# Heads stage without its loop over tiles, and two loads of FP4 codes issued by ScalarE

## The reference, cut to what matters

```python
x = x + cross_attention(layernorm(x), ctx, ctx)        # 512 wide, 256 context rows per sequence
x = x + self_attention(layernorm(x))                   # 16 heads of 128, rotary, causal, 64 tokens per sequence
x = x + ffn(layernorm(x))                              # FP4 weights, 1408 hidden, silu gate, RMS norm of the output
```

## Time and profile before

| what | value |
|---|---|
| median of 3 runs | 1446.46 us (1444.58 to 1448.53) |
| profiled execution | 1445.04 us |
| its span, first to last instruction | 1443.2 us |
| TensorE busy | 1360.7 us (94%), 8964 matmuls |
| VectorE busy | 980.1 us (68%) |
| ScalarE busy | 508.1 us (35%) |
| GpSimd busy | 425.7 us (29%) |
| DMA | 122.53 MB, mean 85 GB/s |
| mean granted TensorE clock | 0.980 of full speed |

### The profile page before, as it was taken

The page is one execution under the profiler, slowest core; times in us unless marked ns, Lnnn a source line. Parts: engine busy times, 40 slices in busy tenths (PEclk is TensorE's granted clock), DMA queues, the critical chain, the costliest instruction groups (busy, mean ns, idle before and its releaser), DMA issues. The chain is left out here.

```text
span 1443.2 us, 24076 instructions
## 1 busy us (share of the span) xinstructions
PE 1360.7 (94%) x8964; PEld 795.3 (55%) x8964; DVE 980.1 (68%) x2176; ACT 508.1 (35%) x1249; POOL 425.7 (29%) x302
## 2 busy tenths in 40 slices
PE   8999999968999899998999999999998499999997
PEld 6666666435666566665667666654443234343433
DVE  6443443447887688776877777738829796969693
ACT  3222222322333333332343333320001483838281
POOL 0000000003333133331333333320302391929292
PEclk9999999989999999999999999999999699999999
DMA  8555555331001100101010000268550000000000
GB/s 323 218 212 211 212 196 193 118 126 54 31 28 47 61 30 31 59 16 60 31 59 30 18 28 31 89 199 244 166 157 1 0 2 29 0 29 0 29 1 30
DMA packets 59459, 122.53 MB, mean 85 GB/s; under 512 B 4312, under 2 KB 37720, under 8 KB 52696
## 3 DMA queue, kind: packets, MB, share of 16 engines
q1 hardware_dynamic: 59352, 121.07, 24.5%
HBM read 95.89 MB, written 25.17 MB: 84 GB/s over the span
## 5 line engine op out<-in xcount | busy, mean ns | idle before, releaser
L931 POOL TENSOR_TENSOR hd_rotated<-hd_products 64x512 f32<-64x512 f32 x64 | 109.3, 1708 | 725.1 <-DVE hd_products L1116 725.1
L184 PE MATMUL psum<-hd_xt_hi,hqk_hi 128*128 128x512 f16 x512 | 195.8, 382 | 1.7 <-DVE hd_xt_lo L1090 1.7
L185 PE MATMUL psum<-hd_xt_lo,hqk_hi 128*128 128x512 f16 x512 | 195.6, 382 | 0.0
L186 PE MATMUL psum<-hd_xt_hi,hqk_lo 128*128 128x512 f16 x512 | 195.2, 381 | 0.0
L1442 POOL TENSOR_TENSOR ff_part<-ff_part 128x512 f32<-128x512 f32 x88 | 127.7, 1465 | 98.0 <-DVE ff_part L1569 97.6
L184 PE MATMUL psum<-hd_wv_hi,hd_xt_hi 128*128 128x256 f16 x512 | 140.3, 274 | 4.6 <-DVE hd_wv_lo L1095 4.6
L1471 PE MATMUL psum<-ff_xt_hi,gu 128*128 128x512 f16 x352 | 133.9, 380 | 8.2 <-DVE w_rows L1607 3.3
L185 PE MATMUL psum<-hd_wv_lo,hd_xt_hi 128*128 128x256 f16 x512 | 140.3, 274 | 0.0
L186 PE MATMUL psum<-hd_wv_hi,hd_xt_lo 128*128 128x256 f16 x512 | 140.2, 274 | 0.0
L1472 PE MATMUL psum<-ff_xt_lo,gu 128*128 128x512 f16 x352 | 133.4, 379 | 0.0
L1569 DVE SCALAR_TENSOR_TENSOR ff_part<-psum,gu_scale,ff_part 128x512 f32<-128x512 f32 x176 | 119.8, 738 | 6.2 <-ACT ff_part L1519 3.6
(11 more groups left out here) (170 smaller groups left out, 2795.0 us busy)
## 6 DMA issues: line engine op xcount, KB each, us to landing
xa_kv_t<-in_ctx_t_dram SPq DMA_DIRECT2D x16, 1024.0 KB, 5.3
xa_kv<-in_ctx_dram SPq DMA_DIRECT2D x16, 1024.0 KB, 4.8
w_rows<-in_head_weights_dram SPq DMA_DIRECT2D x12, 1024.0 KB, 7.5
z_scratch<-hd_z_hi SPq DMA_DIRECT2D x32, 256.0 KB, 2.2
z_scratch<-hd_z_lo SPq DMA_DIRECT2D x32, 256.0 KB, 2.5
w_rows<-z_scratch SPq DMA_DIRECT2D x8, 1024.0 KB, 8.0
hqk_lo<-z_scratch SPq DMA_DIRECT2D x8, 1024.0 KB, 7.7
xn<-in_x_dram SPq DMA_DIRECT2D x8, 512.0 KB, 3.8
```

The costliest lines, as they stand in the source:

```text
L184: pe.matmul(out, lh, rh, start=(first and i == 0), stop=False)
L185: pe.matmul(out, lh, rl, start=False, stop=False)
L186: last = pe.matmul(out, ll, rh, start=False, stop=(final and i == k - 1))
L931: pool.tensor_tensor(rotated[0:HALF, w, 0, :], products[0:HALF, w, 0, :], products[0:HALF, w, 2, :], ALU.subtract)
```

## The change

The heads stage is written out for all four tiles: `for_each_step` no longer takes an engine and has no `Fori`, addresses and counts become constants, and the `nop`s that followed register waits go. In the merge stage the loads of codes 2 and 3 leave SyncE's list and stand at the head of ScalarE's, each behind its wait on `gu_decoded`; SyncE keeps codes 1 and all of z. No arithmetic changes.

```diff
@@ heads_phase
-        def for_each_step(eng, step):
+        def for_each_step(step):
...
-            with eng.Fori(0, NT - 1) as t:
-                tile(t, False)
-            tile(NT - 1, True)
+            for t in range(NT):
+                tile(t, t == NT - 1)
...
-                    sp.nop(nofuse=True)
-                    sp.dma_start(xn[:, :, :], rows_of(s.t * TILE + TILE)).then_inc(x_loaded, 16)
+                    sp.dma_start(xn[:, :, :], rows_of(s.t * TILE + TILE)).then_inc(x_loaded, 16)
                 for h in range(2):
                     banks.wait_moved(sp, s.runs_z, (s.z, h))
-                    sp.nop(nofuse=True)
...
                     banks.wait_moved(pool, s.runs_proj, ("qk"[w], 1))
-                    if not isinstance(s.t, int):
-                        pool.nop(nofuse=True)
...
                     banks.wait_filled(dve, s.runs_scores, s.scores)
-                    dve.nop(nofuse=True)
...
-            for_each_step(nc.tensor, step)
+            for_each_step(step)
@@ merge_phase, sync
-            def load_codes(g):
-                sp.dma_start(codes[g % 2], codes_of(gu_codes, g)).then_inc(gu_loaded[g % 2], 16)
...
             load_z(1, 0)
-            load_codes(1)
+            sp.dma_start(codes[1], codes_of(gu_codes, 1)).then_inc(gu_loaded[1], 16)
...
                 for half in range(2):
                     sp.wait_ge(z_used[half], t - 1 + half)
                     load_z(t, half)
-                    if half == 0:
-                        sp.wait_ge(gu_decoded, t - 1)
-                        load_codes(t)
@@ merge_phase, scalar
+            for g in range(2, KD):
+                act.wait_ge(gu_decoded, g - 1)
+                act.dma_start(codes[g % 2], codes_of(gu_codes, g)).then_inc(gu_loaded[g % 2], 16)
             for n, (_, _, _, hi, _) in enumerate(jobs):
```

More of the change, by code:

```diff
@@ L825, in rows_of @@
         def rows_of(first):
-            return x1_rows[bass.ds(first, TILE), :].rearrange("(b p) d -> p b d", p=P)
+            return x1_rows[first:first + TILE, :].rearrange("(b p) d -> p b d", p=P)
         class Step:
@@ L894, in load_wo @@
                 sp.wait_ge(w_lo_done, t + KD)
-                sp.nop(nofuse=True)
-                sp.dma_start(w_rows[:, 0, :], w_o[:, bass.ds(t * (4 * D), 4 * D)]).then_inc(loaded[0], 16)
+                sp.dma_start(w_rows[:, 0, :], w_o[:, t * (4 * D):(t + 1) * (4 * D)]).then_inc(loaded[0], 16)
             def step(s):
@@ L909, in step @@
                     banks.wait_moved(sp, s.runs_z, (s.z, h))
-                    sp.nop(nofuse=True)
                 for half, z in enumerate((z_hi, z_lo)):
-                    sp.dma_start(z_scratch[half, s.pair * 2:s.pair * 2 + 2, :, bass.ds(s.first_token, TILE)].rearrange("h d t -> d h t"),
+                    sp.dma_start(z_scratch[half, s.pair * 2:s.pair * 2 + 2, :, s.first_token:s.first_token + TILE].rearrange("h d t -> d h t"),
                                  z[:, :, :]).then_inc(small_loaded_z_stored, 16)
@@ L918, in step @@
                         load_wo(s.t + 1)
-            for_each_step(nc.sync, step)
+            for_each_step(step)
         @block.gpsimd
@@ L933, in step @@
                                        ALU.add).then_inc(pool_rotated, 1)
-            for_each_step(nc.gpsimd, step)
+            for_each_step(step)
         @block.tensor
@@ L1065, in step @@
                             act.wait_ge(small_loaded_z_stored, s.a * 32 + 16 * HEADS_SMALL)
-                            act.nop(nofuse=True)
                         act.activation(z_hi[:, h, :], psum_of((s.z, h)), ACT.Identity,
@@ L1076, in step @@
                     act.wait_ge(loaded[0], s.t * 16 + 32)
-                    act.activation(wo_hi[:, bass.ds(s.t * 4, 4), :].rearrange("p n m -> p (n m)"), w_rows[:, 0, :], ACT.Copy,
+                    act.activation(wo_hi[:, s.t * 4:s.t * 4 + 4, :].rearrange("p n m -> p (n m)"), w_rows[:, 0, :], ACT.Copy,
                                    scale=WS).then_inc(wo_hi_done, 1)
@@ L1081, in _ @@
             act.wait_ge(zeros_set, 1)
-            for_each_step(nc.scalar, step)
+            for_each_step(step)
         @block.vector
@@ L1132, in while_exponentials_run @@
                     dve.wait_ge(wo_hi_done, s.t + 1)
-                    if not isinstance(s.t, int):
-                        dve.nop(nofuse=True)
-                    dve.scalar_tensor_tensor(wo_lo[:, bass.ds(s.t * 4, 4), :].rearrange("p n m -> p (n m)"), w_rows[:, 0, :], WS,
-                                             wo_hi[:, bass.ds(s.t * 4, 4), :].rearrange("p n m -> p (n m)"),
+                    dve.scalar_tensor_tensor(wo_lo[:, s.t * 4:s.t * 4 + 4, :].rearrange("p n m -> p (n m)"), w_rows[:, 0, :], WS,
+                                             wo_hi[:, s.t * 4:s.t * 4 + 4, :].rearrange("p n m -> p (n m)"),
                                              ALU.mult, ALU.subtract).then_inc(w_lo_done, 1)
@@ L1164, in step @@
                                                              z_hi[:, h, :], ALU.add, ALU.subtract), (s.z, h))
-            for_each_step(nc.vector, step)
+            for_each_step(step)
 ZW_UNSCALE = 1.0 / (AS * WS)
```

## The result

| kernel | median, us | runs | span of the profiled execution |
|---|---|---|---|
| before | 1445.83 | 1444.58 to 1448.53 (4) | 1443.2 |
| changed | 1428.67 | 1427.44 to 1429.69 (4) | 1425.6 |

The ratio is 0.9878 with a 95% interval of 0.9864 to 0.9892: 17.2 us faster, where 24.8 us were forecast. The time lies 0.3 us inside the upper end of the whole range (1406 to 1429), and outside the forecast's own range (1416 to 1427).

What follows compares the result with a forecast made beforehand. TensorE, busy 94% of the span, bounds the kernel, idling at loop jumps and before the last stage. Gains of 11.8 (loop), 11.9 (23.9 less 12 collision) and 1.1 sum to 24.8 us: 1421 us, range 1406 to 1429.

Steps and rivals of the forecast that it cites:

- the forecast's own range: Whole kernel: 1416 to 1427 us, for z stalls of 6 to 17 us in the merge stage; chance 0.52.
- The loop: Heads stage: writing the loop out removes two jumps, 11.8 us; nops and register waits counted at nothing, bound 0 to 2.
- Rival 3: Heads stage: instruction fetching binds in straight code, giving 6 us of the 11.8 back, 1427 us; chance 0.06.
- VectorE and the gap: Merge stage's end: earlier codes 2 and 3 end VectorE's waits; 23.9 us can be had if z arrive as before.
- The collision: Merge stage: earlier codes loads delay z on shared engines and stall TensorE, 12 us in all, leaving 11.9 of 23.9.
- my upper end: Merge stage: work on the half is conserved, codes served first; z stalls 13.1 us, 15 us with low clock.
- the mark of 17: Merge stage: the prediction fails if TensorE's two z waits sum to over 17 us.
- 1018.3: Merge stage: time in us when z of tile 2 lands in the kernel before, base for adding the codes' work.
- Start of the last stage: Last stage's start: with about 1 us idle the clock stays up and ScalarE's four copies come closer, 1.1 us.
- Free sharing: Merge stage: z never stalls TensorE by more than 5 us; stall 1 us, time 1411 us; chance 0.31.
- The second: Only one half works: z stalls 20 us or more, or VectorE is delayed elsewhere; 1430 to 1434 us; chance 0.07.
- The fourth: Slower than before: merge stage's 54 us of shared work takes 54 f, f above 1.42 decides; 1456 at 1.6; chance 0.04.

Runs made afterwards that it cites:

- a: Changed kernel with the loads of codes 2 and 3 back in SyncE's list behind z, heads stage still written out; 1433.43 us.
- c: Changed kernel with ScalarE's two loads bringing only 32 of 2816 columns of codes 2 and 3 (output wrong); 1405.13 us.
- h: Changed kernel with ScalarE's two loads bringing 1408 of 2816 columns of codes 2 and 3 (output wrong); 1411.62 us.
- d: Changed kernel with codes loads turned so the outermost dimension is 16 words, not 8 copies, using all 16 engines; 1406.74 us.
- e: Changed kernel with ScalarE also waiting, before each codes load, for the landing of the z on the way; 1412.94 us.
- f: Changed kernel with each codes load cut into 11 loads of 256 columns, in 1 KB packets; 1419.25 us.
- g: Changed kernel with codes loads on 16 engines, but groups 2 and 3 back in SyncE's list behind z; 1426.64 us.
- b: Changed kernel with the heads stage's loop and nops restored, codes 2 and 3 still on ScalarE's queue; 1443.22 us.

## Why the prediction was right or wrong

**The loop (11.8 us forecast): right, low by 1.3.** The windows of the two looped tiles lost 5.9 and 6.5 us, all but 0.8 us of the stage's 13.1. The rest is 154.49 to 153.82 us in the third tile and 0.14 in the last. I take these 0.8 us, and what the second window lost beyond 5.9, for the nops and register waits that I counted at nothing with a bound of 2 us; no run takes them out alone. That the loop brings this is shown by a, where it alone gives 12.3 us. Rival 3 (fetching binds in straight code) is out: every window is busy to its full length. A caution for reading single spans here: the first z store falls between 350.88 (c) and 355.72 us (h) in the kernels with the loop written out, before any of the edits acts, while from that store to the last the time is 592.8 us in all of them. So two whole spans can differ by some 5 us for nothing; differences are taken here inside a stage, or between medians.

**VectorE and the gap (23.9 us to be had): right.** The waits for groups 2 and 3 are gone and the gap is 1.05 us. c and d show the size: where no z is waited for, the stage takes 146.3 us, 24.2 less than 170.46.

**The collision (12 us forecast): right in mechanism, 21.2 us in size. This is the step that failed:** the term "12 us in all". Conservation on eight engines with the codes served first was my upper end, 13.1 us of waits and 15 with the clock, and I took less than that. The mechanism is what happened: c, h and d tie the wait to what the loads carry and to the eight engines, and the codes' work measured 12.8 us a load. The waits of 17.56 us are also past the mark of 17 that I had named as a sign of failure, and they came the other way round: 0 to 4 and then 5 to 13 us forecast, 14.2 and then 3.4 measured. Three things were too small.

First, even the upper end puts the z of tile 2 6 us too early: 1018.3 - 13.2 + 2 x 12.8 = 1030.7 us, where the matmul that waited for it started at 1036.65. Kernel c shows where the difference lies, as it has the same issues and next to none of the bytes. Its two loads of this z, issued from 994.35 on (windows 994 to 994.6, the first alone, and 994 to 995.4, both; count, KB each, median us to landing):

```profile
w_rows<-z_scratch SPq DMA_DIRECT2D x1, 1024.0 KB, 6.5
...
w_rows<-z_scratch SPq DMA_DIRECT2D x2, 1024.0 KB, 7.7
```

A median of 7.7 over two, of which one is 6.5, puts the other at 8.9 us: issued near 994.8, it lands at 1003.7, 51.0 us after the stage's first z load (952.67). My 1018.3 is 49.9 us after its own (968.36), so the base of my sum was only 1.1 us early. In the changed kernel the same z comes 1036.65 - 955.16 = 81.5 us after the first load, 30.5 later than in c, for 25.6 us of codes' work. The other kernels with a wait for this z say the same in kind: 14.2 us later than in c for 11.0 us of work in h (q10 has 9.2% of 60 us), 17.6 for 11.4 in e (one load, 16.3% of 35 us), 22.8 for 19.9 in f. So adding up the work gave most of the delay and fell short by 3 to 6 us in each. Why isn't settled.

The landing in the kernel before can't serve as the base of this sum. The load issues from 1010 to 1010.45 (the first of the two z loads) and from 1010 to 1011 (both):

```profile
w_rows<-z_scratch SPq DMA_DIRECT2D x1, 1024.0 KB, 8.1
...
w_rows<-z_scratch SPq DMA_DIRECT2D x2, 1024.0 KB, 10.5
```

By the same working the first lands at 1018, which is the fall of the DMA share that I had read, and the second at 1023.3. But group 2 is issued at 1011.08 right behind them in the same queue, so this landing holds a part of the codes' work already, and 1023.3 - 13.2 + 25.6 = 1035.7, though it comes near the 1036.65, counts that part twice. How far such a landing can move shows in a, whose merge stage is that of before: there this z lands 60.8 us after the stage's first z load and not 54.9 (issued near 998.9, 9.7 us for the first load and a median of 14.2 over both).

Second, in the first wait I had put group 2 alone ahead of the z of tile 1: 1001.5 - 13.2 + 12.8 = 1001.1 us. It landed at 1011, with group 3 too, issued at 995.98, ahead of a part of it. What SyncE's queue gets beside a load of codes is in the changed kernel's queues over 984 to 990 us (packets, MB, share):

```profile
q10 hardware_dynamic: 67, 0.75, 45.3%
q1 hardware_dynamic: 67, 0.08, 5.9%
```

Each queue moved 67 packets. That is what turns packet by packet give, and with packets of 11,264 bytes against 1,024 and 2,048 that gave the codes nine times the bytes. I had weighed turns by time and a larger part for SyncE's queue against codes first, and no row of before could show turns by packet. f agrees: with codes in 1 KB packets the first wait falls from 14.2 to 3.0 us. Where the z is waited for matters less for the total: a wait at the z of tile 1 moves TensorE's need for the z of tile 2 later by as much.

Third, the low clock was paid twice, 3.6 us and not 2. The window of TensorE after the shorter wait (3.35 us), and the columns as in the earlier trace rows:

```profile
1038.00:1041.00 3.00, 3.00 (x8) 1.06 (x7) 2.86 (x6) 0.00 (x0) 0.94 (x1) 0.50 1.00 316
```

PEclk is 0.50, the lower level of 1.2 GHz, one to four us after a wait of 3.35 us.

By these numbers 23.15 + 0.8 - 17.56 - 3.6 = 2.8 us stands where I had 11.9. That the time is still inside the whole range is in part luck: the heads stage gave 13.1 us and not 11.8, and without these 1.3 us the time would have been 1430.

**Start of the last stage (1.1 us forecast): right**, 1.2 us by the spans.

**The rivals.** Free sharing (0.31, 1411 us) is out: the waits sum to 17.6 us, not under 5. The second, that the queue's half is worth nearly nothing (z stalls 20 us or more, 1430 to 1434), was closest in kind: 17.6 us of waits and 3.6 of clock come to 21.2, and the time missed its lower end by 1.3 us. It deserved more than 0.07. What I had in hand for it was the row I used, 65 GB/s for everything else with a codes load on the earlier trace rows. The fourth (slower than before, from a factor of 1.42 on) is out: its own sum, 989 + 54 f + 1.7 - 1030.75, gives f = 1.07 for the 17.6 us of waits and 1.13 with the clock.

**The rule on eight engines.** That a leading broadcast of 8 confines a transfer to 8 engines is in the Trainium skill, "DMA: Bandwidth & Descriptors", "Rules for kernel authors". The traces agree, with shares of 0.51 and 0.52, against 0.97 and 1.06 in d, and d is worth 22 us. The same page of the Trainium skill, "Issuing engines are not separate DMA queues", says that loads from several engines interleave on the same 16 and only issue time is saved. The traces bear this out for the codes' work (12.8 us of eight engines from ScalarE's queue, and by its rate from SyncE's) and not for the end: taking the codes out of the queue in which they stood behind waits for TensorE is worth 19.9 us at 16 engines (g against d).

**What stays open.** Why the z are later than the added work, by 3 to 6 us, isn't settled, nor why the z of tile 1 was held until TensorE had waited 21.5 us in b and 14.2 in the changed kernel. In b this wait alone sets the time, as TensorE comes for the z of tile 2 only at 1054.13, after it has landed. That the turns go by packet is read from one stretch of the changed kernel and from f; f also issues 11 loads for one, which takes ScalarE 14.06 us, and a kernel with large packets in many loads wasn't run. And VectorE's 11.49 us wait for GpSimd is told but not tested: GpSimd's adds wait 62.66 us for the x1 rows of tiles 2 and 3, that stand behind the held z in SyncE's queue, and the wait is gone where z isn't held, in c and d.

## What to carry to other kernels

Before moving a load to another queue, look at which engines it runs on (DMA share and GB/s in a stretch where it is alone), how large its packets are, and what it would run beside. Add its whole work to the landing of what it meets, and take the sum as the least to expect: here 25.6 us of work made the z 30.5 us late. A landing serves as the base only if the moved load isn't in it already. Then mend the load before the queue: the same bytes on 16 engines and not 8 turned a move worth 4.8 us into one worth 19.9 (g against d), 26.7 with what the wider load gives by itself. Where this can't be done, holding the moved load back behind the urgent one (15.7 us) or cutting it into packets of the other's size (9.4 us) is the next best. A loop's jump on an engine that is busy throughout costs what the windows between its turns show, here 5.9 and 6.5 us of TensorE, of which 4.7 are idle time in the one that was looked at.

## What the runs showed of the hardware that was not expected

- Two queues moved the same number of packets beside each other, 67 each in 6 us, one with packets of 11,264 bytes and the other of 1,024 and 2,048. With codes in 11,264-byte packets beside z in 1 KB packets, the z landed 34.5 us after its issue, against 11.7 in the kernel before. With codes in 1 KB packets TensorE's wait for that z is 3.0 us and not 14.2.
- The same 2.88 MB, read eight times over the same words, took 25.6 us of eight engines in 11,264-byte packets and 19.9 in 1,024-byte ones.
- Issue instructions of SyncE were held while codes loaded beside its queue: 14.06 us for two z loads (1.10 before), 18.32 for eight loads of scales of 16 KB (4.45 before). The next z was issued at 1020.13 for it, 23.3 us after its buffer was free.
- VectorE's small operations beside a busy GpSimd. In the kernel before, within a run of GpSimd adds, and in the changed kernel with GpSimd idle, the same line on 128x4 elements:

```profile
1007.79 14.75 POOL L1279 TENSOR_TENSOR hqk_hi<-hqk_hi,hqk_lo 128x512 f32<-128x512 f32 x12 [32.90 <-DMA hqk_hi<-x_scratch]
...
1021.37 1.19 DVE L128 TENSOR_TENSOR ln_y<-ln_y 128x4 f32<-128x4 f32 x1
1022.59 0.16 DVE L129 SCALAR_TENSOR_TENSOR ln_y<-ln_y,ln_var 128x4 f32<-128x4 f32 x1
```

```profile
1000.24 0.16 DVE L128 TENSOR_TENSOR ln_y<-ln_y 128x4 f32<-128x4 f32 x1
```

1.19 us against 0.16: the nine small operations that VectorE runs from 1011.58 to 1021.37, while GpSimd adds (1007.79 to 1022.54), take 1.18 or 1.19 us each, seven times as long, and the first one behind GpSimd's last add takes 0.16 again. The four passes over 128x512 ahead of them took 2.47 us in both kernels.
